# Four graph layers on sixteen graphs: last-layer masks shared by VectorE and GpSimd, a second feature buffer, a projection copied by transfers, and new orders

## The chip, the cores and the metric

One core of a Trainium2 chip runs the whole program. The time is the device time of one launch in microseconds (us). The kernel before takes 2634.27 us, the median of three runs (2633.69 to 2635.55).

## What is computed

Sixteen independent graphs (B = 16) of N = 1024 nodes with D = 128 features, and a 0/1 adjacency of 1024x1024 each, go through four layers. Every layer is `x = layernorm(x + layer(x, adj))`:

```
layer 0   h = x W;  softmax over neighbours of leaky_relu(s_i + t_j);  relu(attention @ h)
layer 1   8 heads of 16 features, same shape of score, elu at the end
layer 2   one relation: (adj / degree) @ x @ W1 + x @ self_w.T + self_b, layernorm * gamma + beta, relu
layer 3   4 heads of 32 features:  Wh = x W
          scores = Wh Wh^T / sqrt(32), masked where adj == 0;  softmax;  attn @ Wh
```

The change is in layer 3 above all. Since a masked score adds nothing to numerator or denominator, the mask can be laid on before the exponential (a very negative number is added to the score) or behind it (the exponential is multiplied by 0 or 1).

## The kernel before

The transposed adjacency of three graphs lies in SBUF as `AT` (128 x 3 x 8 x 1024, bf16). The work is a software pipeline over the graphs. In one period four graphs are in work at once: graph `n` does layer 0 and prepares layer 1, `f = n-1` does layer 1 and prepares layer 2, `k = n-2` does layer 2's sum and layer 3, `m = n-3` is normalised and stored. Each engine has its own table of numbers (`ON_PE`, `ON_ACT`, `ON_DVE`, `ON_POOL`): a period runs over 444 steps, and a piece of work is issued at the step at which its table has it. So the tables are nothing but the order of the pieces on each engine; semaphores carry the dependencies, and an engine that waits holds up all that stands behind it. SyncE issues its transfers in a fixed order written out in `period`.

**Layer 3** is done in 16 couples `v` of two tiles `w = 2v, 2v+1` (two heads). Couple `v` handles two blocks of 128 source nodes, `J = v % 4`, for one half of the target nodes.

- `layer3_scores` (L746 to L769, TensorE) puts the scores of both tiles into four banks of PSUM. For a couple that is not in `MASKED` it first multiplies the mask in: four matmuls `big x AT` of 128x512 in bf16 (L759), with `AT` holding adj - 1, add the negative number where there is no edge. For a couple in `MASKED` these four are left out.
- `layer3_exp` (L1000, ScalarE, L1006) takes each tile from PSUM to one of the four slots of `weight3`.
- `layer3_masked` (L1421, VectorE, L1427) does for both tiles of a couple in `MASKED` the operation `weight3 = (AT + 1) * weight3`. `MASKED` is couples 10 to 14; for the last graph all 16.
- `layer3_values` (L771, TensorE, L783) multiplies both tiles with the projected features and gives the two slots free. The exponential of couple `v + 2` waits for that.
- `layer3_mask` (L1416, VectorE, L1419) turns the whole third of `AT` from adj to adj - 1, once per graph, before the first couple.

Scores of two source blocks run from two copies of the projection, `wT[:, 0]` and `wT[:, 1]`, the second with the halves of the partitions exchanged. The second copy is computed by the matrix `rhs3_far` (L731 in part, L736) in `layer3_project` and `layer3_project_rest`, and brought out of PSUM by `layer3_wide` (L991) in two further copies of 128x512.

`x3`, the input of layer 3, is one buffer: `layer3_residual` of graph `m` (L1448 to L1452), which reads it and takes the statistics of the last norm, must be done before `layer2_norm` of graph `k` (L1392) writes it.

On the way to layer 3 of a graph VectorE does in this order: degree and sum of layer 2 (L1357 to L1364), statistics (L1098 to L1110), `layer3_finish` of graph `m` (L1440, L1444), the affine norm (L1115, L1379, L1381), relu and statistics, `layer3_residual` of graph `m`, the norm into `x3` (L1115), `layer3_mask`, the lengths of the projected rows (L1398 to L1402), their maxima and `shift3` (L1414). Masks of layer 1 (L1290), sums per head (L1298) and some ramps (L1276) stand between them.

GpSimd does the small power `(var + eps) ** -0.5` of every norm (L514, 128x8) and issues the load of the next adjacency, cast to bf16, into memory (L522). SyncE issues all other transfers, among them the transposing load of `AT` (`turn_adjacency`), which waits until layer 3 of the graph three back is through with its third of `AT`.

## Time and profile before

| | |
|---|---|
| median of three runs | 2634.27 us |
| profiled execution, first to last instruction (span) | 2633.3 us |
| profiled execution against the three runs | its time is the span; 1.0 us under the median |
| TensorE busy | 2370.0 us, 90% |
| VectorE busy | 2178.8 us, 83% |
| ScalarE busy | 1961.1 us, 74% |
| GpSimd busy | 156.0 us, 6% |
| mean granted TensorE clock | 0.950 of full |

PE is TensorE's matmuls and PEld its weight loads, which overlap; DVE is VectorE, ACT ScalarE, POOL GpSimd, SP SyncE; a q behind a name is its sequencer or queue. An f32 matmul counts as two instructions. Rows show how long an engine was busy, how long it waited and for whom. Names of tiles leave numbers out: `weight` is `weight0` or `weight3`, `AT` the adjacency, `kp` and `fp` the two parts of PSUM, `shared` holds `wT`.

### The profile page before, as it was taken

The page shows a single profiled execution, that of the slowest core. Times are in us where ns is not written, and L with a number is a line of the kernel's source. Part 1 is how long each engine was busy: PE and PEld are TensorE (multiplying, and loading weights), DVE is VectorE, ACT ScalarE, POOL GpSimd, SP SyncE. Part 2 cuts the span into 40 slices and gives each one's busy share as a digit, 9 for nine tenths or more (in the row PEclk, how much of TensorE's full clock was granted, in tenths as well). Part 3 has the DMA queues.
Part 4 walks back from the last instruction along what each step waited for, and adds up shares of the span by engine and source line. Part 5 has one row for each costly group of instructions (what it writes and reads, how often), then busy time and mean ns, then how long its engine had stood idle before and what let it go on. Part 6 is the DMA issues. An engine that isn't in the chain of part 4 may idle for free.

```text
span 2633.3 us, 56947 instructions
## 1 busy us (share of the span) xinstructions
PE 2370.0 (90%) x23877; PEld 1568.4 (60%) x23877; DVE 2178.8 (83%) x4097; ACT 1961.1 (74%) x2193; POOL 156.0 (6%) x104
## 2 busy tenths in 40 slices
PE   3668998999999999999989899999989999998966
PEld 3658565575756557575655757556575755657331
DVE  3689798897979889798888979788897978989656
ACT  2748787777879777787977778787777878777724
POOL 0000000000000000000000000000000000000000
PEclk9779999999999899999999999999999999999978
DMA  5504041221414223041322304032130403101000
GB/s 124 121 25 122 25 113 42 73 74 34 97 33 98 57 65 81 15 116 33 90 65 58 89 9 122 33 82 73 47 98 11 122 33 82 41 26 42 9 1 17
DMA packets 190417, 164.42 MB, mean 62 GB/s; under 512 B 136656, under 2 KB 170576, under 8 KB 189136
## 3 DMA queue, kind: packets, MB, share of 16 engines
q1 hardware_dynamic: 188864, 127.22, 17.3%
q0 software_dynamic: 1296, 33.56, 6.3%
q8 instruction: 188, 3.08, 0.5%
q14 instruction: 69, 0.57, 0.1%
HBM read 151.78 MB, written 42.53 MB: 74 GB/s over the span
## 4 chain that ended last, share of the span: by engine, by line
PE 46%; DVE 28%; ACT 14%; issue 10%; DMA 1%; SPq 1%; POOL 0%; ACTq 0%; POOLq 0%; DVEq 0%
PE kp L783 13%; PE kp L766 9%; ACT ramp L959 9%; PE fp L605 9%; DVE weight L1290 8%; PE kp L759 6%; PE fp L666 4%; ACT weight L1006 3%; DVE bstat L1098 2%; DVE vh L1298 2%; PE fp L559 1%; PE fp L552 1%; DVE yb L1364 1%; PE fp L684 1%; DVE weight L1427 1%
## 5 line engine op out<-in xcount | busy, mean ns | idle before, releaser
L959 ACT ACTIVATE ramp<-s1row,tbig 128x1024 bf16<-128x1024 f32 x864 | 922.6, 1145 | 72.6 <-DVE weight L1290 70.4
L1006 ACT ACTIVATE weight<-kp,shift 128x1024 f32<-128x1024 f32 x512 | 545.7, 1110 | 271.4 <-PE kp L766 269.9
L1290 DVE TENSOR_TENSOR weight<-ramp,AT 128x2048 bf16<-128x2048 bf16 x512 | 612.3, 1220 | 106.6 <-ACT ramp L959 61.3
L666 PE MATMUL fp<-vh_parts,weight 128*128 128x102 bf16 x8192 | 457.2, 215 | 88.8 <-DVE weight L1290 58.6
L666 PEld LDWEIGHTS fp<-vh_parts,weight 128*128 128x128 bf16 x8192 | 413.8, 101 | 190.5 <-DVE weight L1290 95.7
L783 PE MATMUL kp<-weight,w 128*33 128x512 f32 x2048 | 489.0, 600 | 11.4 <-DVE weight L1427 10.9
L766 PE MATMUL kp<-shared 32*128 32x512 f32 x2048 | 299.7, 655 | 7.9 <-ACT weight L1006 7.5
L783 PEld LDWEIGHTS kp<-weight,w 128*33 128x33 f32 x2048 | 97.8, 110 | 313.2 <-issue 247.4
L605 PEld LDWEIGHTS fp<-h,weight 128*128 128x128 f32 x2048 | 234.5, 194 | 40.0 <-issue 27.8
L605 PE MATMUL fp<-h,weight 128*128 128x129 f32 x2048 | 240.3, 279 | 16.2 <-DVE weight L1203 16.2
L1427 DVE SCALAR_TENSOR_TENSOR weight<-AT,weight 128x1024 f32<-128x1024 bf16 x182 | 214.6, 1221 | 44.2 <-ACT weight L1006 44.2
L647 PE MATMUL kp<-vh_parts,AT 128*128 128x136 bf16 x3072 | 230.5, 237 | 0.0
L1203 DVE SCALAR_TENSOR_TENSOR weight<-weight,v,AT 128x1024 f32<-128x1024 f32 x128 | 161.4, 1283 | 72.1 <-ACT weight L909 71.6
L647 PEld LDWEIGHTS kp<-vh_parts,AT 128*128 128x128 bf16 x3072 | 219.8, 102 | 0.2
L909 ACT ACTIVATE weight<-xfT,v0neg,v0s 128x1024 f32<-128x1024 f32 x128 | 156.7, 1240 | 58.2 <-PE fp L605 55.5
L759 PE MATMUL kp<-AT,big 128*128 128x512 bf16 x660 | 188.3, 404 | 3.1 <-ACT weight L1006 2.9
L711 PE MATMUL kp<-elu,AT 128*128 128x128 bf16 x2048 | 181.4, 221 | 0.0
L708 PE MATMUL kp<-y_hi,AT 128*128 128x129 bf16 x1024 | 178.0, 222 | 3.7 <-DVE elu L1349 3.7
L766 PEld LDWEIGHTS kp<-shared 32*128 32x128 f32 x2048 | 83.0, 189 | 151.3 <-issue 92.9
L1298 DVE TENSOR_REDUCE vh<-fp 128x272 f32<-128x816 f32 x128 | 128.2, 1002 | 43.5 <-PE fp L666 43.5
L711 PEld LDWEIGHTS kp<-elu,AT 128*128 128x128 bf16 x2048 | 159.6, 98 | 0.2
L514 POOL TENSOR_TENSOR bsmall<-bsmall,half_neg 128x8 f32<-128x8 f32 x32 | 67.3, 2102 | 1002.3 <-DVE bsmall L1110 1002.3
(184 smaller groups left out, 2575.9 us busy)
## 6 DMA issues: line engine op xcount, KB each, us to landing
s1row<-s_rows_dram SPq DMA_DIRECT2D x128, 512.0 KB, 4.2
adj_bf_dram<-in_adj_dram POOLq DMA_DIRECT2D x15, 2048.0 KB, 13.3
x<-in_x_dram SPq DMA_DIRECT2D x16, 512.0 KB, 7.2
xfT<-s_row_dram SPq DMA_DIRECT2D x16, 512.0 KB, 5.6
out_dram<-elu SPq DMA_DIRECT2D x16, 512.0 KB, 3.2
adj_bf_dram<-in_adj_dram POOLq DMA_DIRECT2D x2, 1024.0 KB, 10.3
s_rows_dram<-weight SPq DMA_DIRECT2D x16, 32.0 KB
AT<-adj_bf_dram SPq DMA_TRANSPOSE x17, 10.9
```

Of the source, the lines that this page charges most:

```text
L605: last = pe.matmul(fp[:, g, n * (D + 1):(n + 1) * (D + 1)], weight0[:, jt % P0_RING, t * P:(t + 1) * P], h0[:, jt, :], start=(jt == 0 and ...
L647: last = pe.matmul(kp[:, SUM_A_BANKS[t // PER], n * H1 * C1:(n + 1) * H1 * C1].rearrange("p (h c) -> p h c", h=H1), AT[:, third, jt, t * P ...
L666: last = pe.matmul(fp[:, 1 + t // 4, col:col + 2 * PARTS * C1], edges[:, u % B_RING, t * P:(t + 1) * P], vh_parts[:, jt, h, :, :, :].rearr ...
L711: last = pe.matmul(kp[:, g, col:col + D], lhsT, y2_lo[:, jt, k, :], start=False, stop=(jt == T - 1 and k == 1), skip_group_check=True)
L759: pe.matmul(kp[:, 1 + 2 * (w % 2) + x, :], big[:], AT[:, third, 2 * J + x, n * HALF:(n + 1) * HALF], start=True, stop=False, skip_group_ch ...
L766: last = pe.matmul(kp[:, 1 + 2 * (w % 2) + x, :], mine[:, jt * P:(jt + 1) * P], mine[:, n * HALF:(n + 1) * HALF], start=v in masks(b), sto ...
L783: last = pe.matmul(kp[side(h), 0, :], w3[:, (2 * J + x) * H3 + h, :], weight3[:, w % P_RING, x * HALF:(x + 1) * HALF], start=(J == 0 and x ...
L959: act.activation(ramp[:, u % R_RING, :], s1row[:, h % S_RING, :], ACT.Relu, bias=tbig1[:, jt, h:h + 1], scale=BIG).then_inc(ramp_ready.sem, 1)
L1006: act.activation(weight3[:, w % P_RING, :], kp[:, 1 + 2 * (w % 2):3 + 2 * (w % 2), :].rearrange("p a n -> p (a n)"), ACT.Exp, bias=shift3[ ...
L1290: dve.tensor_tensor(edges[:, u % B_RING:u % B_RING + 2, :], ramp[:, u % R_RING:u % R_RING + 2, :], AT[:, third, jt:jt + 2, :], ALU.min).th ...
L1298: dve.tensor_reduce(sumB[:, :, h, :, :].rearrange("p t a c -> p t (a c)"), parts, AX_X, ALU.add) \
L1427: dve.scalar_tensor_tensor(out=mine, in0=AT[:, third, 2 * J:2 * J + 2, n * HALF:(n + 1) * HALF], scalar=1.0, in1=mine, op0=ALU.add, op1=AL ...
```

## The change

- `MASKED` is now every odd couple, eight of sixteen. Such a couple's first tile is multiplied by `AT` (0 or 1) on VectorE, its second on GpSimd, each with a plain `tensor_tensor`. Two semaphores take the place of one. Odd couples are just those with `J` 1 or 3, so `layer3_mask` has to turn only half of the blocks to adj - 1; for the last graph, where all 16 couples are masked this way, it is left out.
- `rhs3_far` and its matmuls are gone. `wT[:, 1]` is copied from `wT[:, 0]` by two transfers of 64 x 1024 f32 between SBUF partitions, issued by SyncE (`spread_far`).
- `x3` has two buffers, so `layer3_residual` may stand behind the norm.
- `h0` and `h1` are laid over one another in `features`; their columns of ones are written anew for each graph.
- The order of every engine comes from new tables, SyncE now among them; a period has 109 steps.

```diff
-    MASKED = (10, 11, 12, 13, 14)
+    MASKED = tuple(v for v in range(16) if v % 2)
...
-        h0 = sb("h0", [P, T, D + 1])
+        features = sb("features", [P, T * H1 * C1])
+        h0 = features[:, 0:T * (D + 1)].rearrange("p (t d) -> p t d", t=T)
+        h1 = features[:].rearrange("p (t h c) -> p t h c", t=T, h=H1)
...
-        x3 = sb("x3", [P, T, D])
+        x3 = sb("x3", [P, 2, T, D])
...
+            def spread_far(b):
+                sp.wait_ge(wT_ready.sem, wT_ready.of(b))
+                for side in range(2):
+                    sp.dma_start(wT[(1 - side) * P // 2:(2 - side) * P // 2, 1, :],
+                                 wT[side * P // 2:(side + 1) * P // 2, 0, :]).then_inc(far_loaded.sem, 16)
...
+            def layer3_masked(b, third, v):
+                w = 2 * v + 1
+                _, n, J = unit3(w)
+                pool.wait_ge(exp3_ready.sem, exp3_ready.of(b, w + 1))
+                mine = weight3[:, w % P_RING, :].rearrange("p (x n) -> p x n", x=2)
+                pool.tensor_tensor(mine, mine, AT[:, third, 2 * J:2 * J + 2, n * HALF:(n + 1) * HALF], ALU.mult) \
+                    .then_inc(pool_masked3.sem, 1)
...
-                for bank, weights, n in ((0, rhs3, 0), (1, rhs3, 1), (2, rhs3_far, 0)):
-                    last = pe.matmul(kp[:, bank, :], weights[:], x3T[:, n * HALF:(n + 1) * HALF], start=True, stop=True)
+                for n in range(2):
+                    last = pe.matmul(kp[:, n, :], rhs3[:], x3T[:, n * HALF:(n + 1) * HALF], start=True, stop=True)
...
-                    pe.wait_ge(mask3_made.sem, mask3_made.of(b))
+                    if b < NB - 1:
+                        pe.wait_ge(mask3_made.sem, mask3_made.of(b))
                     pe.wait_ge(wT_ready.sem, wT_ready.of(b))
+                    pe.wait_ge(far_loaded.sem, far_loaded.of(b))
...
-                    pe.wait_ge(masked3_ready.sem, masked3_ready.of(b, 2 * masks(b).index(v) + 2))
+                    pe.wait_ge(vector_masked3.sem, vector_masked3.of(b, masks(b).index(v) + 1))
+                    pe.wait_ge(pool_masked3.sem, pool_masked3.of(b, masks(b).index(v) + 1))
...
-                if x == 0:
-                    copy(wT[:, 0, :], kp_pair).then_inc(wT_ready.sem, 1)
-                    copy(wT[:, 1, 0:HALF], kp[:, 2, :])
-                else:
-                    copy(wT[:, 1, HALF:N], kp[:, 0, :]).then_inc(wT_ready.sem, 1)
+                copy(wT[:, 0, :], kp_pair).then_inc(wT_ready.sem, 1)
...
-                dve.tensor_scalar(AT[:, third], AT[:, third], -1.0, None, ALU.add).then_inc(mask3_made.sem, 1)
+                product = AT[:, third].rearrange("p (j x) n -> p j x n", j=T // 4)[:, :, 0:2, :]
+                dve.tensor_scalar(product, product, -1.0, None, ALU.add).then_inc(mask3_made.sem, 1)
...
-                for w in (2 * v, 2 * v + 1):
-                    _, n, J = unit3(w)
-                    dve.wait_ge(exp3_ready.sem, exp3_ready.of(b, w + 1))
-                    mine = weight3[:, w % P_RING, :].rearrange("p (x n) -> p x n", x=2)
-                    dve.scalar_tensor_tensor(out=mine, in0=AT[:, third, 2 * J:2 * J + 2, n * HALF:(n + 1) * HALF],
-                                             scalar=1.0, in1=mine, op0=ALU.add, op1=ALU.mult).then_inc(masked3_ready.sem, 1)
+                w = 2 * v
+                _, n, J = unit3(w)
+                dve.wait_ge(exp3_ready.sem, exp3_ready.of(b, w + 1))
+                mine = weight3[:, w % P_RING, :].rearrange("p (x n) -> p x n", x=2)
+                dve.tensor_tensor(mine, mine, AT[:, third, 2 * J:2 * J + 2, n * HALF:(n + 1) * HALF], ALU.mult) \
+                    .then_inc(vector_masked3.sem, 1)
...
-        ON_POOL = dict(rstd2=37, rstd_tail=376, rstd3=196, adjacency=99, rstd_f=442, rstd0=414)
+        ON_POOL = [
+            (dict(adjacency=9, masked3=[2, 3, 5, 6, 7, 8, 10, 11, 13, 14, 15, 17, 18, 19, 20, 21], rstd0=12, rstd1=16,
+                 rstd2=0, rstd3=1, rstd_tail=4),),
```

Three places in the orders follow, each from the middle of the program. The first is VectorE from the end of the relu's statistics (graph `k`) to the norm into `x3`; `elu<-elu,x` is the residual of graph `m`, `tstat` and `tsmall` its statistics, `vh<-fp` a sum of layer 1. Before:

```order
L1290 TENSOR_TENSOR weight<-ramp,AT 128x2048 x2
L1450 TENSOR_TENSOR elu<-elu,x 128x1024
L1098 BN_STATS tstat<-elu 128x6 x8
L1101 TENSOR_TENSOR tsmall<-tstat 128x8
L1102 TENSOR_TENSOR tsmall<-tstat 128x8
L1103 TENSOR_TENSOR tsmall<-tstat 128x8
L1105 TENSOR_SCALAR tsmall<-tsmall 128x8
L1106 TENSOR_SCALAR tsmall<-tsmall 128x8
L1107 SCALAR_TENSOR_TENSOR tsmall<-tsmall 128x8
L1110 TENSOR_TENSOR tsmall<-tsmall 128x8
L1298 TENSOR_REDUCE vh<-fp 128x8x34
L1115 TENSOR_SCALAR x<-yb,bsmall 128x128 x8
```

Now, from the same statistics on:

```order
L1341 TENSOR_REDUCE vh<-fp 128x8x34
L1487 RECIPROCAL rec<-kp 128x12 x2
L1487 RECIPROCAL rec<-kp 128x8
L1491 TENSOR_TENSOR elu<-kp,rec 128x384 x2
L1491 TENSOR_TENSOR elu<-kp,rec 128x256
L1333 TENSOR_TENSOR weight<-ramp,AT 128x2048 x3
L1341 TENSOR_REDUCE vh<-fp 128x8x34
L1160 TENSOR_SCALAR x<-yb,bsmall 128x128 x8
L1333 TENSOR_TENSOR weight<-ramp,AT 128x2048 x2
L1465 TENSOR_SCALAR AT<-AT 128x2x2048
L1319 TENSOR_SCALAR ramp<-s1row,st 128x1024 x2
L1333 TENSOR_TENSOR weight<-ramp,AT 128x2048
```

The residual of `m` with its eight rows is gone from between the statistics and the norm; it stands now behind `shift3`. `layer3_finish` (the reciprocals and `elu<-kp,rec`) stood ahead of the affine norm and now fills the place behind the statistics. The mask over `AT` has half its size.

The second is GpSimd over one period. Before:

```order
L514 TENSOR_TENSOR bsmall<-bsmall,half_neg 128x8
L522 DMA adj_bf_dram<-in_adj_dram 64x16384
L514 TENSOR_TENSOR bsmall<-bsmall,half_neg 128x8
L514 TENSOR_TENSOR tsmall<-tsmall,half_neg 128x8
L514 TENSOR_TENSOR small<-small,half_neg 128x8
L514 TENSOR_TENSOR fsmall<-fsmall,half_neg 128x8
```

Now:

```order
L543 TENSOR_TENSOR bsmall<-bsmall,half_neg 128x8 x2
L566 TENSOR_TENSOR weight<-weight,AT 128x1024
L543 TENSOR_TENSOR tsmall<-tsmall,half_neg 128x8
L566 TENSOR_TENSOR weight<-weight,AT 128x1024 x2
L575 DMA adj_bf_dram<-in_adj_dram 64x16384
L566 TENSOR_TENSOR weight<-weight,AT 128x1024
L543 TENSOR_TENSOR small<-small,half_neg 128x8
L566 TENSOR_TENSOR weight<-weight,AT 128x1024
L543 TENSOR_TENSOR fsmall<-fsmall,half_neg 128x8
L566 TENSOR_TENSOR weight<-weight,AT 128x1024 x3
```

Eight multiplications of 128x1024 (`weight<-weight,AT`) stand between the five small powers, in the exponentials' stretch of the period: three ahead of the next adjacency's load, one behind it, one between the powers of layers 0 and 1, and three to the end. The load has moved from between the first two powers to behind the third multiplication.

The third is SyncE over one period. Before:

```order
L426 DMA x<-in_x_dram 128x8x128
L463 DMA_TRANSPOSE AT<-adj_bf_dram 128x8x1024
L434 DMA s1row<-s_rows_dram 128x1024 x3
L442 DMA s_row_dram<-row 8x128
L434 DMA s1row<-s_rows_dram 128x1024
L446 DMA xfT<-s_row_dram 128x1024
L434 DMA s1row<-s_rows_dram 128x1024
L494 DMA out_dram<-elu 128x8x128
L453 DMA s_rows_dram<-weight 8x1024
```

Now:

```order
L449 DMA s1row<-s_rows_dram 128x1024 x3
L478 DMA_TRANSPOSE AT<-adj_bf_dram 128x8x1024
L449 DMA s1row<-s_rows_dram 128x1024
L441 DMA x<-in_x_dram 128x8x128
L449 DMA s1row<-s_rows_dram 128x1024 x2
L500 DMA shared<-shared 64x1024 x2
L449 DMA s1row<-s_rows_dram 128x1024 x2
L457 DMA s_row_dram<-row 8x128
L461 DMA xfT<-s_row_dram 128x1024
L505 DMA out_dram<-elu 128x8x128
L468 DMA s_rows_dram<-weight 8x1024
```

The two transfers between partitions stand between the source rows of heads 5 and 6, so that these last two rows are issued behind the wait for the projection's copy.

## Rows read from the trace of the kernel before

**Rows 1.** The page, busy time, share of the span and instructions of each engine.

```profile
PE 2370.0 (90%) x23877; PEld 1568.4 (60%) x23877; DVE 2178.8 (83%) x4097; ACT 1961.1 (74%) x2193; POOL 156.0 (6%) x104
```

**Rows 2.** Windows: length, busy PE, PEld, DVE, ACT, POOL; granted clock, DMA share, GB/s.

```profile
235.82:385.90 150.08, 144.22 (x1481) 94.94 (x1479) 126.90 (x225) 122.30 (x138) 7.99 (x5) 0.98 0.24 64
385.90:2399.50 2013.60, 1907.44 (x19417) 1256.08 (x19415) 1743.16 (x3291) 1589.09 (x1781) 124.79 (x77) 0.97 0.24 64
2399.50:2527.52 128.02, 115.77 (x1121) 66.56 (x1118) 87.95 (x174) 75.25 (x78) 7.47 (x5) 0.97 0.05 14
2527.52:2633.30 105.78, 63.32 (x323) 21.04 (x323) 68.46 (x133) 40.17 (x41) 7.67 (x4) 0.81 0.04 11
```

**Rows 3.** Windows, same columns: one period in its parts A, B, C, D.

```profile
1314.80:1352.30 37.50, 29.61 (x383) 26.07 (x382) 36.92 (x82) 24.73 (x32) 6.36 (x4) 0.96 0.33 72
1352.30:1402.60 50.30, 50.13 (x439) 29.51 (x438) 36.73 (x45) 37.99 (x38) 0.00 (x0) 0.96 0.11 34
1402.60:1443.10 40.50, 39.85 (x230) 14.20 (x228) 35.71 (x83) 32.34 (x40) 3.27 (x2) 1.00 0.24 67
1443.10:1469.10 26.00, 25.00 (x433) 24.20 (x432) 23.70 (x39) 26.00 (x28) 0.00 (x0) 1.00 0.48 108
```

**Rows 4.** Chain of waits, one period, in order of time: start, us, what.

```profile
1178.29 1.66 DVE tstat L1098 x8
...
1238.22 9.13 PE fp L605 x80
```

**Rows 5.** Groups of instructions: line, engine, shapes, count; busy us, mean ns; idle before.

```profile
L1427 DVE SCALAR_TENSOR_TENSOR weight<-AT,weight 128x1024 f32<-128x1024 bf16 x182 | 214.6, 1221 | 44.2 <-ACT weight L1006 44.2
L759 PE MATMUL kp<-AT,big 128*128 128x512 bf16 x660 | 188.3, 404 | 3.1 <-ACT weight L1006 2.9
...
L1419 DVE TENSOR_SCALAR AT<-AT 128x8192 bf16<-128x8192 bf16 x16 | 36.6, 2290 | 0.0
...
L736 PE MATMUL kp<-xbT,rhs_far 128*128 128x512 f32 x32 | 16.6, 600 | 0.0
...
L731 PE MATMUL kp<-xbT,rhs_far 128*128 128x512 f32 x32 | 16.4, 593 | 0.0
```

**Rows 6.** Timeline of VectorE, part A: start, us, then the row as above.

```profile
1308.26 0.29 DVE L1357 TENSOR_SCALAR deg<-kp 128x3 f32<-128x3 f32 x3
...
1329.06 2.36 DVE L1290 TENSOR_TENSOR weight<-ramp,AT 128x2048 bf16<-128x2048 bf16 x2
1331.35 1.21 DVE L1450 TENSOR_TENSOR elu<-elu,x 128x1024 f32<-128x1024 f32 x1
...
1335.08 1.00 DVE L1298 TENSOR_REDUCE vh<-fp 128x272 f32<-128x816 f32 x1
...
1350.79 0.14 DVE L1414 TENSOR_SCALAR shift<-kp 128x4 f32<-128x4 f32 x1
```

**Rows 7.** Timeline of GpSimd, start of the program and the same stretch.

```profile
1.11 0.29 POOL L509 TENSOR_SCALAR_AFFINE_SELECT ident<-ones 128x128 f32<-128x128 f32 x1
...
1329.24 2.57 POOL L514 TENSOR_TENSOR bsmall<-bsmall,half_neg 128x8 f32<-128x8 f32 x1 [12.30 <-DVE bsmall L1110]
1335.24 1.65 POOL L514 TENSOR_TENSOR tsmall<-tsmall,half_neg 128x8 f32<-128x8 f32 x1 [3.43 <-DVE tsmall L1110]
```

**Rows 8.** DMA issues of the page: KB each, median us to landing.

```profile
s1row<-s_rows_dram SPq DMA_DIRECT2D x128, 512.0 KB, 4.2
...
x<-in_x_dram SPq DMA_DIRECT2D x16, 512.0 KB, 7.2
```

**Rows 9.** Timelines of ScalarE, VectorE and TensorE at the end, last graph alone.

```profile
2572.85 2.12 ACT L1006 ACTIVATE weight<-kp,shift 128x1024 f32<-128x1024 f32 x2 [1.37 <-PE kp L766]
...
2574.00 2.36 DVE L1427 SCALAR_TENSOR_TENSOR weight<-AT,weight 128x1024 f32<-128x1024 bf16 x2 [1.13 <-ACT weight L1006]
2577.49 2.36 DVE L1427 SCALAR_TENSOR_TENSOR weight<-AT,weight 128x1024 f32<-128x1024 bf16 x2 [1.12 <-ACT weight L1006]
...
2576.42 1.91 PE L783 MATMUL kp<-weight,w 128*33 128x512 f32 x8 [0.16 <-DVE weight L1427]
```

645 lines of the change are left out of this document (329 added, 316 removed).

## The prediction, made before the changed kernel was run

> **What bounds the kernel now.** I read the busy times first: TensorE is busy for 90% of the span, VectorE for 83%, ScalarE for 74%, GpSimd for 6% [rows 1]. No engine is full, so the next view is the windows. Between the small powers of graph 1 and graph 14 lie 13 equal periods in 2013.6 us, 154.9 us each; ahead of them is one of 150.1 us, behind them the last period with two layers in work, 128.0 us, and an end of 105.8 us [rows 2]. The reader is to see that what a period gains counts 13 times and a bit more, and that the end has its own rules.
>
> One period falls into four parts [rows 3]. **Part A**, 37.5 us, from layer 2's sum to the first scores: VectorE is busy for 36.9 us, TensorE for 29.6 us. **Part B**, 50.3 us, the first eight couples and layer 0's products: TensorE 50.1 us, VectorE 36.7 us. **Part C**, 40.5 us, the last eight couples: TensorE 39.9 us, VectorE 35.7 us. **Part D**, 26.0 us, ramps and layer 2's sum: ScalarE 26.0 us. The chain of waits says the same: in part A it runs over VectorE, statistics of the residual among it, in part B over TensorE [rows 4]. So work saved on TensorE counts in B and C, work saved on VectorE in A, and VectorE has room of 13.6 us in B and 4.8 us in C.
>
> **Part A.** Between the degrees at 1308.26 and `shift3` at 1350.79 VectorE has no gap to speak of [rows 6]. The residual of graph `m`, its statistics and small operations take from 1331.35 to 1335.08 there, 3.7 us [rows 6]; with two `x3` they go behind `shift3`: -3.7 us. The mask over `AT` has half the elements of an operation of 2.29 us [rows 5]: -1.1 us. One sum of layer 1 (1.00 us in rows 6) also goes behind `shift3`: -0.9 us. Masks of layer 1 on the way to `shift3` are ten before and ten after. The new ones-columns of `features` add two fills, which the trace has not on VectorE; between nothing and the 0.29 us of a 128x3 operation [rows 6] I take 0.1 us each. The four far matmul instructions, 33.0 us in 64 [rows 5], 2.1 us per graph, leave TensorE, which has 7.9 us of room in A, and the two copies of 128x512 leave ScalarE, which has 12.8 us: nothing, as VectorE's work covers both.
>
> The second projection copy now comes by two transfers of 256 KB, and the first scores wait for them as well as for `shift3`. Nothing in the trace copies between partitions. The nearest rows are 512 KB transfers that land after 4.2 us in the median (source rows) and 7.2 us (`x`) [rows 8]; a half-size one could also be quicker. In the new order some 11 to 12 us of VectorE work lie between the norm into `x3` and `shift3`, and the projection's copy ends some 7 us behind the norm, so at 4.2 us the transfer comes in about with `shift3`. I take +0.6 us, ends -0.5 us (free) and +3 us (7.2 us). The source rows of heads 6 and 7 stand behind this wait on SyncE; their ramps come after the first scores, so they cost nothing unless the transfer is late too. Part A: -3.7 - 1.1 - 0.9 + 0.2 + 0.6 = **-4.9 us**.
>
> **Parts B and C, TensorE.** A masked couple saves four mask matmuls, 188.3 / 660 = 0.285 us each [rows 5], 1.1 us. Of couples 0 to 7 none was masked, now four are: TensorE's B goes from 50.1 to 45.6 us. Of couples 8 to 15 five were, now four: C goes from 39.9 to 41.0 us.
>
> **Parts B and C, VectorE and GpSimd.** A mask of one tile on VectorE cost 1.22 us [rows 5]; `tensor_tensor` has the same shape and one source less to compute, so I keep 1.2 us. In B VectorE gets four of them (4.8 us), the residual (3.7) and the sum (0.9): 36.7 becomes 46.1 us. In C ten become four: 35.7 becomes 28.5 us.
>
> GpSimd's multiplication is in no row. The power of 128x8 takes 1.65 us [rows 7], a lower end. The selection of 128x128 takes 0.29 us [rows 7]; eight times the columns make 2.3 us, and twice that, for two sources, 4.6 us is the upper end. I take 2.3 us, as the row that is nearest in kind (a pass over many columns) gives it. Eight in a period are 18 us of an engine that is 94% idle, so its own time is covered.
>
> What isn't covered is that the two engines hold one another up. The trace shows it once in each period: the power at 1329.24 takes 2.57 us, and beside it VectorE runs two masks of layer 1, which read two operands from SBUF; the power at 1335.24, with a sum out of PSUM beside it, takes 1.65 us [rows 6, 7]. So a GpSimd instruction was late by 0.9 us, nearly one mask. That VectorE is held up in turn doesn't show, since the power reads 8 columns. For a GpSimd multiplication of 2.3 us the price on VectorE lies between nothing and 2.3 us. I take 1.2 us, the middle: part of it meets sums out of PSUM or VectorE's own waits. In B that is 4 x 1.2 = 4.8 us: 46.1 + 4.8 = 50.9 us, now above TensorE's 45.6, against a part of 50.3 us: **+0.7 us**. In C 28.5 + 4.8 = 33.3 us stays under TensorE's 41.0 us: **+0.9 us** for one more product and a little waiting. D changes in nothing that bounds it.
>
> The Trainium skill (SBUF — State Buffer, Who interferes with whom) goes further: the port pair is locked for a whole instruction and the loser fully blocks. This trace agrees as far as it can, 2.57 against 1.65 us on GpSimd's side; by the rule alone B would get up to 9.2 us instead of 4.8. On the multiplication itself, the Trainium skill (GPSIMD Engine Reference, Elementwise — side-by-side cycle accounting) has 4497 ns for 2048 f32 columns, from which I estimate 2.3 us for 1024; no run here shows it yet.
>
> **The end.** With the last graph alone two couples make a round: exponentials (2572.85), both masks on VectorE (2574.00, 2.36 us), values at 2576.42; the masks come every 3.49 us [rows 9]. Now GpSimd starts with the second exponential's end at 2574.97 and needs 2.3 us, to 2577.3 instead of 2576.36. That is 1.0 us more per round and 8 rounds: **+8 us**, with ends +3 us (1.65 us, hardly longer than now) and +26 us (4.6 us). The whole-third mask that is left out there lies beside the turning of `x3`: nothing.
>
> **The sum.** A period: -4.9 + 0.7 + 0.9 = -3.3 us. Thirteen: -43 us. The one ahead: -3 us; the 128 us one, without layer 0: -2 us; the end: +8 us. 2633.3 - 43 - 3 - 2 + 8 = 2593 us, and the median of the runs is 1.0 us above the profiled execution: **2594 us**, 1.5% less. A difference of 0.2%, 5 us, is about what a measurement of this kernel can tell from none.
>
> **Rivals.**
> 1. *VectorE is blocked for the whole of each GpSimd multiplication* (slower). Place: part B, where VectorE's 46.1 us leave little room. Price: 4 x 2.3 us make 55.3 us, +5.0 us; GpSimd starts 0.9 us late behind VectorE's masks and delays values in C, +2.5 us with the extra product; A still gives -4.9 us: +2.6 us a period, +34 in thirteen, +5 in the two others, and 8 x 2.0 = +16 us at the end: 2689 us. It decides from about 2.0 us lost per multiplication. For it: the 2.57 us, and that most of VectorE's work in B reads two operands from SBUF. Against it: not all does, and VectorE has waits there that a block can fall into.
> 2. *The two hardly meet* (faster). B then goes by VectorE's 46.1 us and TensorE's 45.6 us, with 0.6 us of waits: -3.6 us; C +0.4, A -4.9: -8.1 us a period, -105; with -12 beside and +6 at the end 2523 us. For it: the new order puts residual and masks where VectorE waited. Against: the same 2.57 us.
> 3. *The transfers come late*, landing after 7.2 us as `x` does: A gives only -1.9 us, a period -0.3 us, and with +11 at the end (8 and 3) some 2640 us, all but no change. For it: they share queue and engines with source rows of 512 KB. Against: the DMA share in part A is 0.33 [rows 3].
>
> **Chances.** The forecast 0.50, with 2560 to 2625 of its own; rival 1 0.20; rival 2 0.17; rival 3 with others of its size 0.13, of which half is no change and a quarter on either side. Faster: 0.50 + 0.17 + 0.03 = 0.70; same 0.07; slower 0.20 + 0.03 = 0.23. The range 2520 to 2675 takes in rival 2 and rival 3 and most ways to rival 1; some 2 in 10 lie outside, more of it above.
>
> **What would show it.** GpSimd's multiplications at 2.2 to 3.2 us; VectorE's masks of layer 1 no longer 1.22 us in the mean but longer, or gaps in front of them, in B and C only. From the degrees to `shift3` some 37 instead of 42.5 us. In B VectorE over 95% busy and TensorE under 92%. At the end masks every 4.0 instead of 3.49 us. I am wrong if VectorE's rows keep their lengths and waits beside GpSimd's (rival 2), if B is over 54 us (rival 1), or if the first scores wait for the transfers (rival 3).

## The result, and the profile after

The changed kernel takes 2670.69 us in the median of four runs (2667.99 to 2673.03), the kernel before 2633.98 us beside it: ratio 1.0139, 95% interval 1.0125 to 1.0153. It is **slower by 1.4%**; the prediction said 2594 us. The page of the changed kernel, busy time:

```profile
PE 2264.4 (85%) x23543; PEld 1528.5 (57%) x23633; DVE 2274.3 (85%) x4078; ACT 1949.9 (73%) x2161; POOL 527.7 (20%) x240
```

Beside [rows 1], TensorE lost 106 us of work, as meant. VectorE should have lost work too, but it is busy for 96 us more. The windows that answer to [rows 2] (same columns), and under them one period in the parts of [rows 3]:

```profile
231.28:383.68 152.40, 135.68 (x1459) 91.69 (x1465) 134.38 (x224) 121.48 (x136) 30.05 (x14) 1.00 0.26 67
383.68:2421.47 2037.79, 1817.94 (x19154) 1224.26 (x19232) 1839.83 (x3290) 1579.35 (x1755) 421.35 (x182) 0.98 0.26 66
2421.47:2556.52 135.05, 111.53 (x1094) 64.47 (x1098) 94.37 (x172) 76.88 (x77) 25.96 (x13) 0.96 0.07 21
2556.52:2670.70 114.18, 63.67 (x321) 21.89 (x320) 54.99 (x116) 39.35 (x39) 42.41 (x20) 0.78 0.05 14
...
1324.42:1357.74 33.32, 26.93 (x381) 24.90 (x383) 32.39 (x67) 25.32 (x32) 4.19 (x2) 1.00 0.16 41
1357.74:1408.54 50.80, 44.58 (x431) 28.80 (x433) 49.69 (x66) 38.55 (x39) 12.32 (x5) 1.00 0.32 79
1408.54:1456.74 48.20, 42.92 (x234) 15.20 (x235) 36.41 (x79) 34.21 (x42) 15.92 (x7) 0.96 0.10 35
1456.74:1481.21 24.47, 24.41 (x434) 24.05 (x432) 23.08 (x46) 23.40 (x25) 0.00 (x1) 1.00 0.62 150
```

Against the kernel before, thirteen periods cost 24.2 us more, the one ahead 2.3, the last with two layers 7.0, the end 8.4; the start gives back 4.5: together 37.4 us, the difference of the spans. In the one period part A is shorter (33.3 against 37.5 us), B about as long, and **part C is 48.2 us instead of 40.5**, while VectorE is busy there for hardly longer than before (36.4 against 35.7 us) and TensorE for 42.9 of 48.2.

Groups of instructions of the changed kernel (the columns of [rows 5]):

```profile
L566 POOL TENSOR_TENSOR weight<-weight,AT 128x1024 f32<-128x1024 f32 x136 | 345.9, 2544 | 1291.5 <-ACT weight L1053 1291.5
...
L1473 DVE TENSOR_TENSOR weight<-weight,AT 128x1024 f32<-128x1024 f32 x136 | 169.9, 1250 | 93.1 <-ACT weight L1053 93.0
L1341 DVE TENSOR_REDUCE vh<-fp 128x272 f32<-128x816 f32 x128 | 128.1, 1001 | 3.0 <-PE fp L721 2.9
L812 PE MATMUL kp<-AT,big 128*128 128x512 bf16 x390 | 108.9, 382 | 40.6 <-DMA shared<-shared 24.7 <-ACT weight L1053 5.7 <-issue 4.9
...
L1353 DVE TENSOR_TENSOR vh_rest<-vh_rest,c 128x1088 f32<-128x1088 f32 x16 | 46.1, 2883 | 0.5
...
L1146 DVE TENSOR_TENSOR small<-stat 128x8 f32<-128x8 f32 x16 | 25.9, 1620 | 0.6
L1280 DVE TENSOR_SCALAR tdiag<-ident,tcol 8x8 f32<-8x8 f32 x16 | 25.5, 1592 | 0.6
L1465 DVE TENSOR_SCALAR AT<-AT 128x4096 bf16<-128x4096 bf16 x15 | 18.5, 1234 | 0.0
```

GpSimd's multiplication takes 2.54 us in the mean (2.11 undisturbed, 4.11 at most). Three VectorE groups stand out: a product of 128x1088 (`vh_rest`) at 2883 ns, and two instructions of 8 columns at 1.6 us. Before they took 1292 ns (`vh_rest`), 172 (`small`) and 219 (`tdiag`). Timelines of part C, GpSimd and then VectorE, show why:

```profile
1413.82 2.11 POOL L566 TENSOR_TENSOR weight<-weight,AT 128x1024 f32<-128x1024 f32 x1 [17.72 <-ACT weight L1053]
...
1424.63 2.17 POOL L566 TENSOR_TENSOR weight<-weight,AT 128x1024 f32<-128x1024 f32 x1 [5.29 <-ACT weight L1053]
...
1434.79 2.69 POOL L566 TENSOR_TENSOR weight<-weight,AT 128x1024 f32<-128x1024 f32 x1 [2.60 <-ACT weight L1053]
1444.17 2.16 POOL L566 TENSOR_TENSOR weight<-weight,AT 128x1024 f32<-128x1024 f32 x1 [6.68 <-ACT weight L1053]
1452.19 2.57 POOL L566 TENSOR_TENSOR weight<-weight,AT 128x1024 f32<-128x1024 f32 x1 [5.86 <-ACT weight L1053]
```

```profile
1412.46 1.65 DVE L1143 BATCH_NORM_STATS2 stat<-x 128x6 f32<-128x128 f32 x8
1414.14 1.83 DVE L1146 TENSOR_TENSOR small<-stat 128x8 f32<-128x8 f32 x1
1415.89 0.16 DVE L1147 TENSOR_TENSOR small<-stat 128x8 f32<-128x8 f32 x1
...
1425.53 2.35 DVE L1377 SCALAR_TENSOR_TENSOR yf<-elu,yf 128x1024 f32<-128x1024 f32 x1 [0.72 <-ACT elu L1015]
...
1435.72 1.79 DVE L1280 TENSOR_SCALAR tdiag<-ident,tcol 8x8 f32<-8x8 f32 x1
...
1445.13 3.55 DVE L1304 TENSOR_TENSOR vh_rest<-vh,vh_parts 128x1088 f32<-128x1088 f32 x2 [0.78 <-ACT vh_parts L930]
...
1453.06 1.23 DVE L1388 TENSOR_TENSOR yf<-fp,y_hi 128x1024 f32<-128x1024 f32 x1 [0.29 <-ACT y_hi L930]
```

A multiplication that starts at 1413.82 ends at 1415.93, and the VectorE instruction that began at 1414.14 ends at 1415.97 although its twin behind it needs 0.16 us. The same holds at 1424.63, 1434.79 and 1444.17. One VectorE instruction stands still until GpSimd's ends, whatever its own size; a long one then still does its own work (`yf` at 1425.53 takes 2.35 us, in e2 1.22). Not every instruction is held: the statistics, which read one operand (begun at 1412.46), and the product at 1453.06, which has one operand in PSUM, meet a multiplication and keep their length. All four held ones are links of dependent chains: the statistics of layer 0's norm, the elu of layer 1 ahead of its norm, the shifts of layer 1 and its value parts. The chain of waits runs through the first three:

```profile
1414.14 1.83 DVE small L1146
...
1425.53 2.36 DVE yf L1377
...
1435.72 1.80 DVE tdiag L1280
...
1444.17 2.17 POOL weight L566
...
1452.19 2.58 POOL weight L566
```

In the page's chain VectorE's share rises from 28% to 42% of the span, GpSimd's from 0% to 4%. Two theories followed, and a third that the rows don't exclude. **Theory 1**: the held instructions lengthen VectorE's chain. **Theory 2**: the new order of part C costs by itself. **Theory 3**: latency, which means that TensorE's values wait for GpSimd's slower multiplication (45.5 us in all, 45 times).

### The profile page after: what moved, and what is told of

Same layout as the page of the kernel before. It is cut to its first block, busy times and chain, and to the rows that moved or that the text cites. A ratio compares the mean times of both kernels' runs of the same rounds, so it can differ in the third digit from the quotient of the medians.

```text
span 2670.7 us, 56693 instructions
## 1 busy us (share of the span) xinstructions
PE 2264.4 (85%) x23543; PEld 1528.5 (57%) x23633; DVE 2274.3 (85%) x4078; ACT 1949.9 (73%) x2161; POOL 527.7 (20%) x240
## 4 chain that ended last, share of the span: by engine, by line
DVE 42%; PE 31%; issue 10%; ACT 8%; POOL 4%; DMA 4%; SPq 1%; DVEq 0%; POOLq 0%; ACTq 0%
DVE weight L1333 8%; PE kp L837 5%; PE fp L721 5%; PE kp L766 4%; DVE weight L1244 3%; POOL weight L566 3%; ACT weight L1053 3%; PE kp L702 3%; DMA s1row<-s_rows_dram 3%; PE kp L819 3%; PE fp L660 3%; PE kp L763 2%; ACT ramp L1010 2%; DVE weight L1473 2%; DVE vh_rest L1353 2%
## 5 line engine op out<-in xcount | busy, mean ns | idle before, releaser
L1333 DVE TENSOR_TENSOR weight<-ramp,AT 128x2048 bf16<-128x2048 bf16 x512 | 615.3, 1230 | 26.4 <-ACT ramp L1010 14.8
L566 POOL TENSOR_TENSOR weight<-weight,AT 128x1024 f32<-128x1024 f32 x136 | 345.9, 2544 | 1291.5 <-ACT weight L1053 1291.5
L837 PE MATMUL kp<-weight,w 128*33 128x512 f32 x2048 | 506.7, 616 | 89.5 <-POOL weight L566 45.5
L721 PE MATMUL fp<-vh_parts,weight 128*128 128x102 bf16 x8192 | 431.7, 210 | 83.8 <-DVE weight L1333 44.0
L721 PEld LDWEIGHTS fp<-vh_parts,weight 128*128 128x128 bf16 x8192 | 397.3, 99 | 176.1 <-issue 91.1
L660 PE MATMUL fp<-features,weight 128*128 128x129 f32 x2048 | 240.3, 279 | 46.2 <-DVE weight L1244 46.2
L660 PEld LDWEIGHTS fp<-features,weight 128*128 128x128 f32 x2048 | 234.8, 194 | 70.7 <-DVE weight L1244 36.8
L1473 DVE TENSOR_TENSOR weight<-weight,AT 128x1024 f32<-128x1024 f32 x136 | 169.9, 1250 | 93.1 <-ACT weight L1053 93.0
L960 ACT ACTIVATE weight<-xfT,v0neg,v0s 128x1024 f32<-128x1024 f32 x128 | 155.2, 1236 | 105.7 <-PE fp L660 94.6
L766 PEld LDWEIGHTS kp<-elu,AT 128*128 128x128 bf16 x2048 | 159.6, 98 | 0.2
L812 PE MATMUL kp<-AT,big 128*128 128x512 bf16 x390 | 108.9, 382 | 40.6 <-DMA shared<-shared 24.7
```

What stands on the lines that cost most here:

```text
L566: pool.tensor_tensor(mine, mine, AT[:, third, 2 * J:2 * J + 2, n * HALF:(n + 1) * HALF], ALU.mult) \
L660: last = pe.matmul(fp[:, g, n * (D + 1):(n + 1) * (D + 1)], weight0[:, jt % P0_RING, t * P:(t + 1) * P], h0[:, jt, :], start=(jt == 0 and ...
L721: last = pe.matmul(fp[:, 1 + t // 4, col:col + 2 * PARTS * C1], edges[:, u % B_RING, t * P:(t + 1) * P], vh_parts[:, jt, h, :, :, :].rearr ...
L766: last = pe.matmul(kp[:, g, col:col + D], lhsT, y2_lo[:, jt, k, :], start=False, stop=(jt == T - 1 and k == 1), skip_group_check=True)
L837: last = pe.matmul(kp[side(h), 0, :], w3[:, (2 * J + x) * H3 + h, :], weight3[:, w % P_RING, x * HALF:(x + 1) * HALF], start=(J == 0 and x ...
L1333: dve.tensor_tensor(edges[:, u % B_RING:u % B_RING + 2, :], ramp[:, u % R_RING:u % R_RING + 2, :], AT[:, third, jt:jt + 2, :], ALU.min).th ...
```

## The experiments

For all runs one table: the parts of a period, as means of ten periods read from the timelines. To have the same marks in every kernel, A runs here from the degrees of layer 2 to `shift3`, B to the end of layer 0's products, C to the end of the last values, D to the next degrees. "Second tile" says who masks it. The kernels with "nobody" and e3 leave the second tile unmasked, and e8 multiplies it by the adjacency less one.

| kernel | order | second tile | A | B | C | D | period | median us | ratio to before (95%) |
|---|---|---|---|---|---|---|---|---|---|
| before | old | VectorE | 42.5 | 51.4 | 40.4 | 20.5 | 154.9 | 2634 | |
| after | new | GpSimd | 37.5 | 52.2 | 48.0 | 19.0 | 156.7 | 2670.7 | 1.0139 (1.0125 to 1.0153) |
| e1 | new | VectorE | 37.5 | 49.6 | 45.8 | 19.4 | 152.3 | 2600.3 | 0.9870 (0.9856 to 0.9885) |
| e2 | new | nobody | 37.5 | 47.4 | 42.5 | 20.4 | 147.8 | 2529.7 | 0.9603 (0.9588 to 0.9617) |
| e3 | new | GpSimd, elsewhere | 37.5 | 52.5 | 45.8 | 20.4 | 156.1 | 2661.4 | 1.0115 (1.0096 to 1.0134) |
| e5 | new | GpSimd 1, 3, 5, 7 | 37.5 | 52.1 | 45.8 | 19.4 | 154.9 | 2646.7 | 1.0047 (1.0030 to 1.0065) |
| e6 | new | GpSimd 9 to 15 | 37.5 | 49.5 | 47.7 | 19.0 | 153.7 | 2620.3 | 0.9951 (0.9934 to 0.9967) |
| e7 | new | GpSimd, two halves | 37.5 | 51.4 | 48.7 | 19.0 | 156.6 | 2673.3 | 1.0149 (1.0131 to 1.0167) |
| e8 | old | GpSimd | 42.6 | 51.2 | 46.1 | 20.0 | 159.9 | 2707.2 | 1.0278 (1.0261 to 1.0296) |
| e9 | old | nobody | 42.6 | 51.3 | 40.0 | 20.6 | 154.5 | 2625.8 | 0.9966 (0.9953 to 0.9979) |
| e4 | new | VectorE, 10 to 14 | 38.5 | 48.8 | 52.8 | 19.0 | 159.0 | 2697.5 | 1.0243 (1.0228 to 1.0258) |
| e10 | e1, residual early | VectorE | 42.8 | 49.4 | 45.8 | 19.5 | 157.4 | 2679.4 | 1.0175 (1.0155 to 1.0195) |
| e11 | e1, far matmuls | VectorE | 38.2 | 49.2 | 46.1 | 19.5 | 153.0 | 2606.4 | 0.9890 (0.9875 to 0.9904) |
| e12 | e1, ramps on ScalarE | VectorE | 37.5 | 53.5 | 46.5 | 19.5 | 156.9 | 2671.4 | 1.0136 (1.0121 to 1.0151) |
| e13 | old, two x3 | VectorE | 39.7 | 52.9 | 40.4 | 20.5 | 153.6 | 2616.3 | 0.9931 (0.9916 to 0.9946) |
| e14 | e13, couple 9 too | VectorE | 39.0 | 53.0 | 53.2 | 20.6 | 165.8 | 2793.4 | 1.0604 (1.0589 to 1.0620) |
| e15 | e13, 3 and 5 too | VectorE | 38.9 | 59.8 | 40.4 | 20.5 | 159.6 | 2707.6 | 1.0276 (1.0259 to 1.0293) |

Two things go with part C's length in this table. The first is TensorE's granted clock. In the kernel before, e2 and e9 it is at its upper level (2.4 GHz) through all of part C. In the changed kernel eight of the ten periods have 3.4 us at the lower level (1.2 GHz) there, and part C takes 48.4 us in them against 46.7 in the other two: 1.3 us of the mean of 48.0. The stretch from 1419.1 to 1422.5 us comes after TensorE has waited 2.40 us for a mask. e1 and e3 have it in six of ten periods (46.5 against 44.8 us), e8 in all. No run holds the clock fixed, so that the waits bring it down is read from its place and not shown. The second is the border to part D: in the changed kernel the last values end later, and D is 1.4 us shorter than in e2 and e3. For C and D together the changed kernel has 67.0 us, e3 66.2, e2 62.9 and the kernel before 60.9.

### e1, e2, e3: who masks the second tile

```diff
 e1, on VectorE, and GpSimd's multiplication gone:
+                for w, done in ((2 * v, vector_masked3), (2 * v + 1, pool_masked3)):
 e2, nowhere; e3, GpSimd on yb instead of the tile; in both:
-                    pe.wait_ge(pool_masked3.sem, pool_masked3.of(b, masks(b).index(v) + 1))
+                    pe.wait_ge(exp3_ready.sem, exp3_ready.of(b, 2 * v + 2))
```

> The changed kernel with the second tile of each masked couple on VectorE too; the set of couples, the half mask, the orders, the far transfers and the feature buffers stay. Three theories of why part C takes 48.2 us instead of the 41.4 forecast. Theory 1 (held up): during each GpSimd multiplication one VectorE instruction of the critical chain stands still, about 1.4 us each. Then this kernel trades 8 x 1.4 = 11 us of standing still for 8 x 1.25 = 10 us of masks in a period: C 45 to 48 us, the last graph alone back to the 3.5 us rhythm of the masks (-8 us), in all 2645 to 2665 us. Theory 2 (the new order of part C costs by itself, whoever masks): within 8 us of the changed kernel less the end, 2655 to 2670 us; it tells little from theory 1 here and needs the next two. Theory 3 (latency: the values wait for GpSimd, which takes 2.5 us where VectorE takes 1.25): each late couple comes 1.3 us earlier, C 42 to 44 us, in all 2590 to 2620 us.

> The changed kernel without GpSimd's multiplication; the second tile of each masked couple stays unmasked, so that part of the computation is left out, in the last graph too. VectorE's tile is masked as before. It gives the whole price of the multiplications, held-up time and latency together. Theory 1 (held up) and theory 3 (latency) both expect C at 40 to 42 us and B at 46 to 48 us: -9 to -12 us in each of 13 periods, and the last graph alone 12 to 16 us shorter: 2520 to 2560 us. Theory 2 (the new order of part C costs by itself): C stays at 46 us or more and only B and the end gain: 2600 us or more.

> The changed kernel with GpSimd's multiplication at the same places and of the same shape and types, but on another buffer (yb, idle then), and with TensorE's values waiting for the exponential instead of for it. The second tile of each masked couple stays unmasked, so that part of the computation is left out. The two engines meet as before, but nobody waits for GpSimd. Theory 1 (held up): little changes, the VectorE instructions beside a multiplication stay stretched by 1 to 1.5 us, and the time stays within 15 us of the changed kernel's periods, 2640 to 2665 us, of which some 10 us from the last graph alone. Theory 3 (latency): near the kernel without any multiplication, 2520 to 2570 us. Half of each: 2600 us.

Without any second mask (e2) the kernel takes 2529.7 us: the multiplications cost 141 us, 1.04 us for each of 136. VectorE's own masks (e1) cost half of that, 70.7 us or 0.52 us each, though they take 1.22 us of VectorE apiece and the second tile on GpSimd takes none. The busy time of VectorE says the same from its side: 2105.7 us in e2, 2272.2 in e3, 2274.3 in the changed kernel, so 168.6 us are held time, 1.24 us for each multiplication. e3 settles latency: nobody waits for GpSimd, and only 9 of the 141 us go. Groups of VectorE in e3, and the same two in e2:

```profile
L1357 DVE TENSOR_TENSOR vh_rest<-vh_rest,c 128x1088 f32<-128x1088 f32 x16 | 46.2, 2885 | 0.6
L1150 DVE TENSOR_TENSOR small<-stat 128x8 f32<-128x8 f32 x16 | 25.9, 1620 | 0.5
```

```profile
L1352 DVE TENSOR_TENSOR vh_rest<-vh_rest,c 128x1088 f32<-128x1088 f32 x16 | 20.7, 1292 | 0.6
L1145 DVE TENSOR_TENSOR small<-stat 128x8 f32<-128x8 f32 x16 | 2.8, 172 | 0.6
```

The stretched instructions are as long as in the changed kernel though they share no tile with GpSimd: theory 1 stands, theory 3 falls but for its 9 us. At e1 the measured 2600.3 us lay in theory 3's 2590 to 2620 us and missed theory 1's 2645 to 2665, which had priced VectorE's own masks at their full length; e1 alone would have misled, and e3 was needed. By the parts, the multiplications cost B 4.8 us (three of them, 1, 3, 5) and C 5.5 us (five), C and D together 4.1. In part C e1 and e3 are alike (45.8 us): in this order VectorE's own masks cost as much there as the held time does, and what parts the two kernels is B (49.6 against 52.5 us) and D.

### e4: the old masks in the new order

```diff
-    MASKED = tuple(v for v in range(16) if v % 2)
+    MASKED = (10, 11, 12, 13, 14)
```

> The changed kernel with the masking of before: couples 10 to 14 masked, both tiles by VectorE's scalar_tensor_tensor, the mask over the whole third, also for the last graph. Orders, two x3 buffers, far transfers and feature buffers are the changed kernel's. Theory 1 or 3 (GpSimd's multiplications cost what was lost): part A keeps 4 of its 5.4 us of gain, B and C are TensorE's and near those of before (50 and 41 us): 2575 to 2600 us. Theory 2 (the new order of part C costs by itself): C 45 us or more, 2630 to 2660 us.

Part C takes 52.8 us, more than theory 2 had. It was meant to undo the masks, but it put them at places that the new order never fitted: even couples are masked there in the last graph only. TensorE's values wait 117.4 us for masks, against 48.8 in e1. 6.8 us of part C are at the lower clock. So this tells that an order and its set of masked couples belong together, and nothing on theory 2.

### e5, e6: early or late couples

```diff
+                    if k is not None and v in masks(k) and (v < 8 and k < NB - 1) and s == at["masked3"][v]:
```

> The changed kernel with GpSimd multiplying only for couples 1, 3, 5 and 7 and never in the last graph; the second tiles of 9, 11, 13 and 15, and of the last graph, go to VectorE. Part B holds three of the multiplications that are left (1, 3, 5), part C one. Theory 1a (a multiplication costs where it stands, in both parts alike, by the VectorE instruction that it holds up): part B stays at 52 us as in the changed kernel, where both tiles on VectorE gave 49.6, part C comes to 46 us from 48.0; with 2600 us for both tiles on VectorE and 15 periods of +2.5 to +3 us this makes 2635 to 2650 us. Theory 1b (only part C's chain is hurt, part B has room for it): within 5 us of 2600 us plus one multiplication, 2600 to 2615 us.

> The mirror of the run before: GpSimd multiplies only for couples 9, 11, 13 and 15 and never in the last graph, all four in part C; the others' second tiles go to VectorE. Theory 1a (a multiplication costs where it stands): part B 49.6 us, part C 47.5 us against 45.8 with both tiles on VectorE: 2600 + 15 x 1.5 to 2 = 2620 to 2632 us, and the two halves' excesses over 2600 us together with the 8 to 12 us of the last graph add up to the changed kernel's 70 us. Theory 1b (only part C's chain is hurt): nearly the whole loss is here, 2650 to 2662 us.

e5 lies 46 us above e1, e6 20 us. The last graph alone, which neither has on GpSimd, takes 6 us more in the changed kernel than in e1 (114.2 against 107.9 us from its first power on): 72 us, against 70 in all. The loss arises where the multiplication stands, in B (+2.5 us by three) and C (+1.9 us by four), net of the mask that VectorE is spared: theory 1a. The runs of e5 scatter from 2635.0 to 2660.7 us, more than others here; its profile is of the fastest.

### e7: two short instructions for a long one

```diff
+                for x in range(2):
+                    done = pool.tensor_tensor(mine[:, x], mine[:, x], AT[:, third, 2 * J + x, n * HALF:(n + 1) * HALF], ALU.mult)
```

> The changed kernel with each GpSimd multiplication of 1024 columns cut into two of 512 columns, one after the other. If a VectorE instruction that meets one is held until that instruction ends (and not slowed down in proportion), it now gets through at the seam: the stretched instructions end 1.0 to 1.3 us after they began instead of 1.6 to 2.9 us, but the second half can hold another one. Held once per multiplication for half as long: 2630 to 2645 us. Held twice for half as long: 2665 to 2680 us. If each GpSimd instruction has a fixed part of some tenths of a us, the multiplications come to 2.4 to 2.8 us together and the last graph alone gets 2 to 5 us longer: up to 2690 us.

```profile
L567 POOL TENSOR_TENSOR weight<-weight,AT 128x512 f32<-128x512 f32 x272 | 416.0, 1547 | 1258.5 <-ACT weight L1055 1258.5
```

The held instructions got shorter (`tdiag` 1592 to 741 ns, `vh_rest` 2883 to 2026 ns), but others were held instead (`vh_rest<-vh_rest,vh` 1405 to 2079 ns). VectorE's busy time fell by 43 us, to 2231.3. In return two halves take GpSimd 2 x 1547 ns against 2544, and TensorE's waits for it grew from 45.5 to 74.3 us. The time is the same. An instruction is held to the end of the one that it meets, not slowed in proportion; cutting trades held time for latency.

### e8, e9: the same in the old order

```diff
+                pool.tensor_tensor(mine, mine, AT[:, third, 2 * J:2 * J + 2, n * HALF:(n + 1) * HALF], ALU.mult)
...
-                for w in (2 * v, 2 * v + 1):
+                for w in (2 * v,):
```

> The kernel before, with its own order, where only the second tile of the masked couples (10 to 14, all 16 in the last graph) goes to GpSimd, by a multiplication with the third of the adjacency as it stands there (less one, so those tiles are weighted wrongly; the shape, types and places are the same). Theory 1 (held up): VectorE saves 5 x 1.2 = 6 us and loses 5 x 1.4 = 7 us by held instructions in part C, all on its chain: part C 41 to 43 us instead of 40.4; with 8 to 16 us more in the last graph alone 2650 to 2685 us. Theory 2 (it is the new order that makes the multiplications costly): part C stays at 40.4 us or falls by some of the 6 us, and the kernel gains or stays: 2580 to 2640 us.

> The kernel before with its own order, where the second tile of each masked couple (10 to 14, all 16 in the last graph) stays unmasked, so that part of the computation is left out. It completes the square: two orders, each with the second tiles on GpSimd, on VectorE and on nobody. Theory 1 (part C hangs on VectorE's own chain, in which every mask or held instruction counts with about half or more of its length): part C falls from 40.4 by 2.5 to 5 us, 2634 - 15 x (2.5 to 5) - 5 for the last graph = 2555 to 2590 us, and the GpSimd version of this order lies 115 to 150 us above it. The forecast's step (part C is TensorE's, VectorE has room there): part C stays within 0.7 us, 2620 to 2632 us.

This pair names the failed step. VectorE's five second masks in part C cost 0.4 us a period there (40.4 against 40.0), though they are 6 us of work: they are covered, as the forecast had it and against what I wrote under theory 1. Five multiplications on GpSimd, which take nothing from VectorE's work, cost 6.1 us (46.1 against 40.0), 81 us in all. VectorE in e8, then in e9:

```profile
L1276 DVE TENSOR_TENSOR vh_rest<-vh,vh_parts 128x1088 f32<-128x1088 f32 x32 | 95.2, 2975 | 0.0
L1246 DVE TENSOR_SCALAR tbig<-st 128x64 f32<-128x64 f32 x16 | 22.6, 1414 | 0.0
L1442 DVE SCALAR_TENSOR_TENSOR weight<-AT,weight 128x1024 f32<-128x1024 bf16 x91 | 137.9, 1516 | 65.5 <-ACT weight L1021 65.5
L1130 DVE TENSOR_SCALAR x<-yf,fsmall 128x128 f32<-128x128 f32 x128 | 63.5, 569 | 25.7 <-POOL fsmall L516 25.7
```

```profile
L1275 DVE TENSOR_TENSOR vh_rest<-vh,vh_parts 128x1088 f32<-128x1088 f32 x32 | 41.1, 1284 | 0.6 <-ACT vh_parts L893 0.6
L1245 DVE TENSOR_SCALAR tbig<-st 128x64 f32<-128x64 f32 x16 | 3.0, 187 | 0.0
L1441 DVE SCALAR_TENSOR_TENSOR weight<-AT,weight 128x1024 f32<-128x1024 bf16 x91 | 111.4, 1224 | 92.9 <-ACT weight L1020 92.9
```

A mask of VectorE's own stands at a place chosen for it, where VectorE would wait for ScalarE anyway (92.9 us in e9). Held time falls on whatever VectorE has just begun, and that is work of the chain: `vh_rest` loses 1.7 us each time. In all VectorE is busy for 2209.7 us in e8 and 2080.9 in e9, 1.42 us for each of 91 multiplications. But not all of the 6.1 us is held time. VectorE also waits 1.6 us a period for the small power of layer 1's norm, which stands behind a multiplication in GpSimd's order (25.7 us in the last row of e8, nothing in e9); TensorE waits 1.3 us of part C for GpSimd; and 5.5 us of it are at the lower clock, none in e9. The old order has no run like e3, so how the 6.1 us divide stays open. Theory 2 falls as a reason for the held time: the old order pays 1.2 us per multiplication in part C, no less than the new one (1.1). My range for e8 ended at 2685 us, since I set five holds against five masks saved; the masks saved were worth nothing.

### e10, e11: the other parts of the change, undone in e1

```diff
-                 relu2=21, residual3=46, rest2=102, shift0=58, shift3=39, shifts1=91, stats2=16, tail3=64, top0=36,
+                 relu2=21, residual3=25, rest2=102, shift0=58, shift3=39, shifts1=91, stats2=16, tail3=64, top0=36,
```

> Base: the changed kernel with both tiles on VectorE (2600 us). The residual of layer 3 with its statistics (3.7 us of VectorE) goes back from behind the layer-3 shift to a place ahead of the norm that feeds layer 3, as in the kernel before; the second x3 buffer stays. If part A's gain is a true one: part A +3.7 us, part B not shorter: 2650 to 2656 us. If VectorE bounds part B as well (48.8 of its 49.6 us busy in the base), the work only changes its part: A +3.7, B -3 to -3.7 us: 2597 to 2612 us.

> Base: the changed kernel with both tiles on VectorE (2600 us). The second projection copy is made as in the kernel before, by two matmul instructions of 512 columns per graph and two copies on ScalarE, instead of two transfers. The forecast had the transfers' gain covered by VectorE and the wait for them at +0.6 us a period; undoing them gives 2590 to 2600 us by that. If the transfers took load off a chain in part A (TensorE 33.2 of 37.5 us busy there): +1 to +2 us a period, 2612 to 2630 us.

The residual ahead of the norm costs part A 5.3 us and gives part B back only 0.2: it is more than the 3.7 us of work moved, so part A's gain is a true one; the whole loss, 79 us, is more than either range had. And B is not VectorE's alone, though it was busy for 98% of it (48.8 of 49.6 us in e1's window): VectorE's masks wait 120.9 us for exponentials in e10 against 77.2 us in e1. The far matmuls cost 0.7 us in A, 6 us in all, between the two ranges. The ratios, 0.9890 and 0.9870, have intervals that overlap, so the transfers are at most a small gain, where the forecast had a small loss.

### e12: ramps from VectorE to ScalarE

```diff
-    OWN_RAMPS = (4, 8, 21, 24, 27)
+    OWN_RAMPS = (4, 8, 21)
...
-                 ramps=[0, 1, -1, 2, 3, 4, -1, 6, 7, 8, 9, 11, 13, 15, 16, 20, 21, 22, 25, -1, 29, 30, -1, 33, 36, -1,
+                 ramps=[0, 1, -1, 2, 3, 4, -1, 6, 7, 8, 9, 11, 13, 15, 16, 20, 21, 22, 25, -1, 29, 30, 32, 33, 36, 38,
```

> Base: the changed kernel with both tiles on VectorE (2600 us). Two of the five couples of layer-1 ramps that VectorE makes itself (numbers 24 and 27, both in part B, 1.42 us a couple) go to ScalarE (2.3 us a couple), which is busy for 39.9 of part B's 49.6 us. If VectorE bounds part B (48.8 of 49.6 us busy): part B -2 to -2.8 us, 2558 to 2572 us. If ScalarE's exponentials come late because of the ramps: part B unchanged or longer, 2598 to 2620 us.

```profile
DVE weight L1473 <- ACT weight L1053: 159.9, 76, 5.6
```

A miss of both ranges: part B +3.9 us. The row is from the waits of e12 (us in all, times, longest); in e1 it reads 77.2 us. The added ramps stand before exponentials on ScalarE's queue, and VectorE's masks, with all that is behind them, wait for those. Part B also has 3.8 us at TensorE's lower clock, against 0.3 in e1.

### e13, e14, e15: the old order with part A's move, and more masks in it

```diff
-        x3 = sb("x3", [P, T, D])
+        x3 = sb("x3", [P, 2, T, D])
...
-        ON_DVE = dict(mask3=111, finish3=46, residual3=96, out2=42, stats2=46, relu2=70, lengths3=134, maxima3=147,
+        ON_DVE = dict(mask3=111, finish3=46, residual3=157, out2=42, stats2=46, relu2=70, lengths3=134, maxima3=147,
```

> The kernel before with its own orders, masks on VectorE (10 to 14, both tiles), far matmuls; only x3 has two buffers (room for it by laying h0 and h1 over one another, as in the change) and the residual of layer 3 with its statistics stands behind the layer-3 shift. If the gain forecast for part A is true and part B has VectorE time to spare for it (36.7 of 50.3 us busy, TensorE 50.1): part A -3.7 to -5 us, B and C unchanged, 2634 - 15 x (3.7 to 5) = 2559 to 2580 us, less than both kernels. If part B or C gives it back: 2600 to 2634 us, and the loss of the changed kernel would in part be the new place of the residual.

> The run before plus couple 9 masked on VectorE (both tiles), so that six couples of part C are. Part C is TensorE's (39.9 of 40.5 us busy) with VectorE at 35.7 us. If a mask that VectorE makes itself is covered there: TensorE -1.1 us a period, 10 to 17 us less than the run before. If part C hangs on VectorE's chain: 10 to 37 us more.

> The kernel of the run before the last plus couples 3 and 5 masked on VectorE (both tiles), both in part B, where TensorE is busy for 50.1 of 50.3 us and VectorE, with the residual, for some 40.5 us. If covered: TensorE -2.3 us a period, 30 to 35 us less than the kernel with two x3 alone. If the masks hold up the layer-1 work behind them on VectorE's queue while they wait for ScalarE's exponentials: no gain, or up to 35 us more.

Two `x3` in the old order give A -2.8 us, B +1.5, in all -18 us. That is in the second range: the residual is not wholly covered in B. e14 and e15 are large misses. One couple more in C costs 12.8 us of it, two more in B 6.9 us. The waits of e14:

```profile
DVE weight L1429 <- ACT weight L1007: 198.6, 61, 9.9
```

Before, the same wait was 44.2 us. Couple 9's mask stands early in VectorE's table, and there VectorE waits up to 9.9 us for the exponential while layer 0's and layer 1's norms stand behind it. The clock follows: 11.9 us of part C in e14 and 10.6 us of part B in e15 are at the lower level, against none and 1.0 in e13. How much of the loss is the wait and how much the clock stays open, and whether a better place would pay wasn't tried.

**The best version** is e1: the change with both tiles on VectorE, 2600.3 us, 1.3% under the kernel before and 2.6% under the changed one (2600.3 / 2670.7).

## Why the prediction was wrong, step by step

- **Part A, -4.9 us**: right. From the degrees to `shift3` it is 37.5 us in the mean instead of 42.5. The half mask is as priced (1234 against 2290 ns). The fills take 0.07 and 0.11 us. How the 5.0 us divide isn't shown: moving the residual back costs 5.3 us of part A in the new order (e10), moving it away gives 2.8 in the old one (e13).
- **The transfers, +0.6 us**: they land after 3.6 us, `x` after 5.6 instead of 7.2; TensorE waits 24.7 us for them in all, 1.5 us a graph. Against the far matmuls they gain some 0.7 us of part A (e11), so rival 3 is out.
- **GpSimd's multiplication, 2.3 us**: 2.54 in the mean, 2.11 to 2.17 undisturbed. The Trainium skill (GPSIMD Engine Reference, Elementwise — side-by-side cycle accounting), from which an estimate of 2.3 us was also made, agrees within 0.2 us.
- **The lock loss, 1.2 us per multiplication on VectorE**: right. VectorE's busy time gives (2274.3 - 2105.7) / 136 = 1.24 us in the new order and 1.42 in the old one. As a price of the period it is 4.8 / 3 = 1.6 us in B and 4.1 / 5 = 0.8 in C and D together, 1.04 in the mean of the run.
- **Part B, +0.7 us**: right by its sum (+0.8 in the mean), with the terms off on both sides, so part of it is luck. The order and the masks gave 4.0 us (e2 against before), three multiplications took 4.8. The signs came true: VectorE is busy for 49.7 of 50.8 us, TensorE for 44.6.
- **Part C, +0.9 us: the step that failed.** It measured +7.6 us (48.0 against 40.4), with D +6.1. The prediction added 4.8 us of held time to VectorE's 28.5, found 33.3 under TensorE's 41.0, and set it at nothing. But neither engine fills part C: in the changed kernel VectorE is busy for 36.4 and TensorE for 42.6 of 48.0 us, and the chain of waits goes from one to the other and back. So free time on VectorE was no measure of what a held instruction costs. e9 against before shows the gap to be real for masks that stand at a chosen place (0.4 us for five), e8 against e9 shows it to be none for multiplications on GpSimd (6.1 us, of which held time is a part that stays open; in the new order e3 against e2 has +3.3 us of part C with no latency in it).
- **Part C, the count**: the parts were counted wrongly: the table puts values 0 to 5 into part B and 6 to 15 into C, in both kernels, so three masked couples lie in B and five in C, not four and four, and TensorE's work on masks in C stays as it was. Of the 7.6 us 5.5 are the multiplications (after against e2); of these 1.3 come with the lower clock and 1.4 are taken from D. The other 2.1 are the new order's (e2 against before). Most of them are a border too: in the new order six of the eight value matmuls of couple 5 lie behind the end of layer 0's products, which is 1.4 us by the 1.91 us that eight take in [rows 9]. Part B is shorter by as much. The rest, 0.7 us, stays open.
- **The other stretches**: the period ahead +2.3 us instead of -3, the one with two layers +7.0 instead of -2, both by the same multiplications: without them e2 has 146.3 us against 150.1 before, and 123.0 against 128.0. The start, which the sum left out, gives 4.5 us back.
- **The end, +8 us**: +8.4, by luck. The prediction had all of it as latency. In e3, where nobody waits for GpSimd, the end takes 111.7 us against 105.7 in e2 and 114.2 in the changed kernel: 6.0 us are held time and 2.4 us latency. Nor are the places as told: the way to `shift3` is 2.3 us shorter, the first mask starts 6.4 us behind it instead of 2.8, and the 16 first tiles' masks are spread over 59.9 us instead of 53.6, every 3.49 and 4.04 us in turn where the run is steady. The forecast had 4.0 us for each.

```profile
2622.79 1.22 DVE L1473 TENSOR_TENSOR weight<-weight,AT 128x1024 f32<-128x1024 f32 x1 [2.86 <-ACT weight L1053]
2626.28 1.23 DVE L1473 TENSOR_TENSOR weight<-weight,AT 128x1024 f32<-128x1024 f32 x1 [2.27 <-ACT weight L1053]
2630.32 1.23 DVE L1473 TENSOR_TENSOR weight<-weight,AT 128x1024 f32<-128x1024 f32 x1 [2.81 <-ACT weight L1053]
```

- **What would show it**: I had looked for the loss on VectorE's masks of layer 1, and they kept their length (1230 against 1220 ns). It fell on products of 128x1088, on the elu and on the small instructions of the norms.
- **The rivals**: rival 1 (2689 us) was nearest in time, but it put the price into B with 5.0 us and into C with 2.5. Rival 2 (2523 us) is what e2 measures, 2529.7: so much the change would give if GpSimd's multiplications cost nothing. Rival 3's part A counts the 0.6 us twice: it should be -2.5 us and the whole some 2632 us, which changes nothing in how it ends.

## What to carry to other kernels

Before work goes to GpSimd, ask which VectorE instruction will be running beside it, not how busy VectorE is: each 2.2 us multiplication held VectorE for 1.24 us, and the kernel paid 1.04 of that, so idle VectorE time elsewhere paid for little. The same work on VectorE, where it cost 1.22 us of the engine but stood at a fitted place, was half as dear in one order (0.52 us) and all but free in the other (0.3%, 9 us for 91). And when two engines pass a chain back and forth, a part can be longer than either is busy, so the larger busy time is a lower bound and not yet a forecast. Last, moving one set of masks or ramps in a fitted order without its neighbours lost time in all four tries (e4, e12, e14, e15): 3 to 7%, against e1 for the new order and e13 for the old one, with longer waits at the head of a queue and TensorE longer at its lower clock. The residual alone could be moved at a gain (e13, 18 us).

## What the runs showed of the hardware

- A GpSimd multiplication of two SBUF operands holds a VectorE instruction until its own end, however small that is: `tdiag`, 8x8, 219 to 1592 ns; `v0neg`, 128x8, 172 to 1756 ns. The sums out of PSUM kept 1001 ns, the statistics (one operand) 278 ns an instruction, and the product with one operand in PSUM 1225 ns. The Trainium skill (SBUF — State Buffer, Who interferes with whom) has this rule: whoever comes first keeps the shared pair for a whole instruction, the other fully blocks, and a VectorE instruction with two SBUF inputs or in a two-port mode is affected. This trace agrees, and the prediction had weighed the rule; what I had not expected is how often it reaches an instruction of 8 columns in a chain.
- It goes both ways: beside VectorE's products GpSimd's multiplication grew from 2.11 to as much as 4.11 us.
- Half the columns took 1.14 us undisturbed against 2.11 (e7), so a fixed part is small, some 0.2 us (an estimate: 2 x 1.14 - 2.11).
- At the lower clock a value matmul takes 1060 ns instead of 598 in the changed kernel, and a 3.4 us stretch of it makes part C 1.7 us longer (48.4 against 46.7 us).
